# One core, a fused block of embedding, quantised attention, experts and local attention: pairs finished two at a time, a norm turned in two batches with the router's logits second, value moves by tile, and another order before the last projection

## What is computed

```python
h = tok(x)                                   # patches @ W.T + b, class token, positions
h = h + attn0(layernorm(h))                  # 4-bit input, ternary weights, 16 heads
h = h + ffn0(layernorm(h))                   # shared expert + top 2 of 8 experts
h = h + attn1(layernorm(h))                  # attention with a latent, then windowed attention
h = h + clip((layernorm(h) @ sign(w).T) * scale + bias, -100, 100)

def attn0(x):
    proj = quant4(x) @ ternary_weight(Wqkv_w).T + Wqkv_b
    ql, kl = rotary(q) @ U, rotary(k) @ U
    y = softmax(ql @ kl.T / sqrt(dk)) @ v
    return quant4(y) @ ternary_weight(Wo_w).T     # quant4: one scale per token

def ffn0(x):
    probs = softmax(x @ router_w + router_b)      # rw, ids = top 2, weights made to sum to 1
    y = sum over e of w_e * (silu(x @ gate_w[e]) * (x @ up_w[e])) @ down_w[e]
    return y + (silu(x @ sh_gate_w) * (x @ sh_up_w)) @ sh_down_w
```

## Time and profile before

| | |
|---|---|
| median of 3 runs | 330.63 us (328.04 to 330.92) |
| profiled execution | 332.31 us, span 330.3 us, 8349 instructions |
| busy share | PE 94%, PEld 79%, DVE 66%, ACT 49%, POOL 46% |
| chain that ended last | PE 60%, DVE 17%, SyncE's queue 8%, issue 5%, ACT 5%, DMA 2% |
| mean granted clock of TensorE | 0.967 of full |
| DMA | 36.74 MB, mean 111 GB/s |

### The profile page before, as it was taken

One profiled execution on the slowest core, in us unless ns is written; L12 is line 12 of the kernel. 1 busy time (PEld: TensorE's weight loads), 2 busy tenths in 40 slices (PEclk: granted clock), 3 DMA queues, 4 the chain that ended last, 5 costly groups with the idle time before them and its releaser, 6 DMA issues.

```text
span 330.3 us, 8349 instructions
## 1 busy us (share of the span) xinstructions
PE 309.3 (94%) x3406; PEld 260.3 (79%) x3408; DVE 217.0 (66%) x574; ACT 160.4 (49%) x353; POOL 153.1 (46%) x178
## 2 busy tenths in 40 slices
PE   7999999999898898999999999999699998999886
PEld 5775678876588888999999999999575676567765
DVE  1089898997877434455655545453577986898674
ACT  0304575556343135576667676763221694169410
POOL 1201209910334782698879888986582000410020
PEclk9999999998979979999999999999979999999987
DMA  7992001320021252537666566514800000000002
GB/s 267 403 396 92 3 0 57 127 99 2 1 96 50 89 167 83 177 127 240 212 221 203 183 217 206 196 34 119 269 4 0 3 9 5 2 1 9 5 2 73
DMA packets 18879, 36.74 MB, mean 111 GB/s; under 512 B 4602, under 2 KB 12849, under 8 KB 18840
## 3 DMA queue, kind: packets, MB, share of 16 engines
q1 hardware_dynamic: 17440, 33.35, 30.2%
q0 software_dynamic: 960, 2.43, 2.3%
q10 hardware_dynamic: 440, 0.41, 0.5%
HBM read 30.28 MB, written 5.75 MB: 109 GB/s over the span
## 4 chain that ended last, share of the span: by engine, by line
PE 60%; DVE 17%; SPq 8%; issue 5%; ACT 5%; DMA 2%; another core or an unknown queue 1%; POOL 1%; ACTq 0%; DVEq 0%; POOLq 0%
PE ps L1662 13%; PE ps L1663 11%; PE ps L1664 11%; SPq L465 8%; PE ps L1442 4%; PE ps L1860 3%; PE ps L1549 2%; PE ps L1454 2%; PE ps L1449 1%; DMA vo<-v_tok 1%; PE ps L1517 1%; PE ps L1561 1%; DVE stats L789 1%; PE ps L1824 1%; PE ps L1574 1%
## 5 line engine op out<-in xcount | busy, mean ns | idle before, releaser
L1339 POOL TENSOR_TENSOR w0l<-raw,w0h 128x384 fp32r<-128x384 f32 (+1 forms) x60 | 56.3, 975 | 15.7 <-ACT w0h L573 15.3
L1089 DVE TENSOR_TENSOR ps<-gact,ps 128x256 f32<-128x256 f32 (+3 forms) x60 | 26.2, 437 | 40.6 <-ACT gact L592 39.0
L1355 POOL TENSOR_TENSOR rstd<-vtmp,cst 128x3 f32<-128x3 f32 (+1 forms) x8 | 6.7, 840 | 91.3 <-DVE vtmp L799 46.3
L1339 POOL TENSOR_TENSOR w1l<-raw,w1h 128x384 fp32r<-128x384 f32 (+1 forms) x48 | 44.8, 971 | 6.5 <-ACT w1h L573 5.7
L592 ACT ACTIVATE gact<-ps 128x256 f32<-128x256 f32 (+3 forms) x60 | 23.2, 387 | 24.8 <-PE ps L1664 16.5
L1094 DVE TENSOR_TENSOR hrl<-ps,hrh 128x256 fp32r<-128x256 f32 (+1 forms) x48 | 20.3, 423 | 18.5 <-ACT hrh L596 17.6
L596 ACT ACTIVATE hrh<-ps 128x256 fp32r<-128x256 f32 (+1 forms) x48 | 18.5, 384 | 27.2 <-DVE ps L1089 26.0
L1662 PE MATMUL ps<-xg0h,w1h 128*128 128x256 f32 x88 | 25.8, 293 | 0.0
L1662 PE MATMUL ps<-xg1h,w0h 128*128 128x256 f32 x88 | 25.6, 291 | 0.0
L1442 PE MATMUL ps<-cst 128*128 128x512 f32 x54 | 25.3, 614 | 0.0
L1663 PE MATMUL ps<-xg1l,w0h 128*128 128x256 f32 x88 | 24.9, 283 | 0.0
(11 more groups left out here) (309 smaller groups left out, 898.7 us busy)
## 6 DMA issues: line engine op xcount, KB each, us to landing
raw<-in_wexp SPq DMA_DIRECT2D x18, 768.0 KB, 4.3
raw<-in_wexp SPq DMA_DIRECT2D x9, 640.0 KB, 4.4
xg_d<-zero SPq DMA_DIRECT2D x8, 256.0 KB, 10.7
xgs<-xg_d SPq DMA_DIRECT2D x8, 256.0 KB, 4.6
stage_l<-in_xT SPq DMA_DIRECT2D x6, 320.0 KB, 5.0
yg_d<-y SPq DMA_DIRECT2D x7, 256.0 KB
stage_l<-in_tokW SPq DMA_DIRECT2D x6, 128.0 KB, 5.0
stage_l<-in_wq SPq DMA_DIRECT2D x1, 512.0 KB, 5.2
```

The source lines that it names most:

```text
L1089: V.tensor_tensor(up, gact[i % 2][rows_of(c), 0:n], up, ALU.mult).then_inc(S("hm"), 1)
L1339: last = nc.gpsimd.tensor_tensor(wset[i][1][w], raw[w], wset[i][0][w].bitcast(F32), ALU.subtract)
```

## The change

1. Values: SyncE waits ahead of each part of a batch for the tile from which it is read, in place of one wait per group.
2. Pairs: `finish` takes two pairs at once for the pairs 0 to 5 (`FINISH`), so that the stream on VectorE is shift, shift, finish of two; the rounding stays one instruction a pair. The last two pairs are finished singly. The spare products are two instead of four. In the tail two spare products are put ahead of the row scales, and three spare products take the place of the keep-clock product.
3. Last projection: three biases, two keep-clock products, the transposes, three spare products, the fourth bias.
4. Norm of the shared products: turned into four banks (two batches by two halves); `xTh` and `xTl` are made batch by batch, first of all; the copies to `xnT` follow them. Unit 0 starts with the first batch. The logits stand behind unit 0, the position products behind unit 2.

```diff
@@ pe: pairs @@
-                    pe.wait_ge(S("y"), p - 1)
+                    pe.wait_ge(S("y"), p // 2)
...
-                for _ in range(4):
+                for _ in range(2):
...
                 turn_y(p)
-            pe.wait_ge(S("ma7"), PAIRS)
+            spare(2, 5)
+            pe.wait_ge(S("ma7"), len(FINISH))
...
             turn_y(PAIRS - 1)
-            keep_clock(1, 1)
+            spare(3, 5)
@@ vector: pairs @@
+            def finish(first, n):
+
+                done = FINISH.index((first, n)) + 1
+                pairs = slice(first, first + n)
+                dve.wait_ge(S("y_mm"), first + n)
+                yv = bank(6 + first % 2, n).rearrange("p (a c) -> p a c", a=n)[:, :, 0:H * VW].rearrange(
+                    "p a (j w) -> p a j w", w=VW)
+                z = rz[:, first % 2:first % 2 + n, :]
+                link(V.reciprocal(z, yv[:, :, :, DH]))
+                y = yq[:, pairs, :]
+                V.tensor_tensor(y.rearrange("p a (j w) -> p a j w", w=DH), yv[:, :, :, 0:DH],
+                                z.unsqueeze(3).to_broadcast([P, n, H, DH]), ALU.mult).then_inc(S("y"), 1)
+                dve.wait_ge(S("y"), done)
+                m = ma2[:, pairs]
+                link(V.tensor_reduce(m, y, AX_X, ALU.max, apply_absolute_value=True))
+                V.tensor_scalar(m, m, 1e-6, 1.0 / 7.0, ALU.max, ALU.mult).then_inc(S("ma7"), 1)
+                dve.wait_ge(S("ma7"), done)
+                link(V.reciprocal(rma[:, pairs], m))
+                for p in range(first, first + n):
+                    V.tensor_scalar(yq[:, p, :], yq[:, p, :], rma[:, p:p + 1], MAGIC, ALU.mult,
+                                    ALU.add).then_inc(S("yr"), 1)
+
+            for i in range(PAIRS // 2):
+                shift(2 * i)
+                shift(2 * i + 1)
+                if i >= 1:
+                    finish(2 * i - 2, 2)
+            finish(PAIRS - 2, 1)
+            finish(PAIRS - 1, 1)
@@ scalar: norm @@
-            act.wait_ge(S("nT_mm"), 1)
-            A(xnT[:, 0, :], bank(4, 2)[:, 0:TP], ACT.Copy).then_inc(S("nT0"), 1)
-            act.wait_ge(S("nT0"), 1)
-            act.wait_ge(S("nT1"), 1)
-            for k in range(DC):
-                A(xTh[:, k, :], xnT[:, k, :], ACT.Copy).then_inc(S("xTh"), 1)
+            for i in range(2):
+                act.wait_ge(S("nT_mm"), turned_upto(1, i))
+                for k in range(DC):
+                    A(xTh[:, k, cols_of(i)], first_turned(i, k), ACT.Copy).then_inc(S("xTh"), 1)
+            for i in range(2):
+                act.wait_ge(S("xTl"), DC * i + 1)
+                A(xnT[:, 0, cols_of(i)], first_turned(i, 0), ACT.Copy).then_inc(S("nT0"), 1)
@@ vector: norm @@
-            dve.wait_ge(S("nT_mm"), 1)
-            V.tensor_copy(xnT[:, 1, :], bank(6, 2)[:, 0:TP]).then_inc(S("nT1"), 1)
-            for k in range(DC):
-                dve.wait_ge(S("xTh"), k + 1)
-                V.tensor_tensor(xTl[:, k, :], bank(4 + 2 * k, 2)[:, 0:TP], xTh[:, k, :].bitcast(F32),
-                                ALU.subtract).then_inc(S("xTl"), 1)
+            for i in range(2):
+                for k in range(DC):
+                    dve.wait_ge(S("xTh"), DC * i + k + 1)
+                    V.tensor_tensor(xTl[:, k, cols_of(i)], first_turned(i, k), xTh[:, k, cols_of(i)].bitcast(F32),
+                                    ALU.subtract).then_inc(S("xTl"), 1)
+            for i in range(2):
+                V.tensor_copy(xnT[:, 1, cols_of(i)], first_turned(i, 1)).then_inc(S("nT1"), 1)
@@ pe: shared products @@
             transposes(1)
-            spare(4, 0)
-            pe.wait_ge(S("nT0"), 1)
-            pe.wait_ge(S("nT1"), 1)
...
+            def logits():
+                pe.wait_ge(S("nT0"), 2)
+                pe.wait_ge(S("nT1"), 2)
...
             for u in range(NH):
-                if u == 0:
-                    pe.wait_ge(S("xTl"), DC)
+                if u < 2:
+                    pe.wait_ge(S("xTl"), DC * (u + 1))
                 if u >= 2:
                     pe.wait_ge(S("hl"), u - 1)
                 shared_gate_up(u, u // 2, u % 2)
-                if u == 1:
+                if u == 0:
+                    logits()
+                if u == 2:
                     pe.wait_ge(S("sel"), 1)
@@ sync: values @@
-                    sp.wait_ge(S("v_tok"), (TT - MOVED) * li + grp + 2 - MOVED)
-                    if li == 0:
+                    if li == 0 and grp == 2:
                         sp.wait_ge(S("cleared"), 2)
                     for b in range(4 * grp, 4 * grp + 4):
                         for lo, hi in rows_of_batch(b):
+                            sp.wait_ge(S("v_tok"), (TT - MOVED) * li + lo // P + 1 - MOVED)
@@ pe: last projection @@
-            for t in range(4):
+            for t in range(3):
                 pe.wait_ge(S("bn"), TT * 4 + t + 1)
                 bias(t)
+            pe.wait_ge(S("bn"), TT * 4 + 4)
+            keep_clock(2, 3)
             transposes(4)
+            spare(3, 3)
+            bias(3)
```

## The result

The changed kernel took 335.65 us (median of 4 runs, 333.75 to 336.61), the kernel before 330.77 beside it: ratio 1.0154, 95% interval 1.0092 to 1.0217. It is slower, by less than 2%. Timed again in twelve executions on another chip it was slower by less: 328.44 against 326.01 us, ratio 1.0052 (1.0016 to 1.0088). I had forecast 326.8 us, 1% faster. Ratios and averages leave disturbed executions out and medians take all in, so that the two need not agree; three ratios (the short fallback, the old norm with four spare products the first time, the new order alone the first time) stand on 334.0 us for before, where its average beside them is 331.5, and there I go by the averages.

A forecast was written before the change was run, and what follows sets the result against it. VectorE paces the pair loop from pair 4 on, TensorE products the experts, TensorE the last projection. Terms -1.5 - 0.6 + 3.3 - 2.85 - 2.2 = -3.85 against the 330.63 us median give 326.8 us; 8-in-10 range 322.5 to 331.

The forecast's parts named there:

- ScalarE's stall: 4.92 us idle before a SiLU near the scatters: shorter gives 323.5 us, chance 0.18; longer gives 330, chance 0.12.
- Pairs, -1.5: Pair loop: joined finishes save VectorE time, less a hole no longer filled and later values; -1.5 us, bounds -0.7 and -2.2.
- the clock falls inside the pair loop: Rival: fewer spare products and waits for joined divisions halve TensorE's clock; three such pairs give 335.5 us; chance 0.06.
- Tail, -0.6: End of the pair loop: short spare products finish before the copy, so the first output projection isn't held up; -0.6 us.
- Norm and router, +3.3: Norm before the shared products: reordering delays router and position products, hence the scatters; +3.3 us, bounds +1.9 and +3.3.
- Router +1.4: VectorE's first router operation begins at 95.6 instead of 94.18, since the logits come later; +1.4 us.
- Position products behind a half-clock unit 2, +1.9: After 4 us of TensorE idle time unit 2 runs at half clock, so VectorE waits 1.9 us for the position products.
- Values, -2.85: Both local-attention layers: group 2's DMA queue starts earlier, ending TensorE's waits; -1.6 and -1.25 us, bounds -2.3 and -3.0.
- Last projection, -2.2: Final projection: TensorE at full clock, then VectorE sets 0.88 us a tile; last clip at 325.2 instead of 327.34, -2.2 us.
- The clock in the last projection: Rival: the clock goes down there all the same, turning the 2.2 us gain into +0.5; 329.5 us, chance 0.14.

The follow-up runs named there:

- the short fallback: Changed kernel with most products cut from TensorE's never-entered code for experts given more rows than fit: 330.96 us, before 333.70, ratio 0.9886.
- the one with the gap filled: Changed kernel with filler restoring the branch's place and ten spare products in TensorE's idle time ahead of the third shared unit: 325.02 us, ratio 0.9980.
- 34 earlier in before: Kernel before with fewer, equivalent spare products, so its branch lies 34 TensorE instructions earlier, as in the changed kernel: 333.55 us, before 333.70, ratio 1.0037.
- 222 later: Kernel before with 222 more TensorE instructions ahead of its branch, small products replacing three keep-clock products: 332.29 us, before 326.37, ratio 1.0208.

## Why the prediction was wrong

**What failed** is the way in which the sum was made: I counted what each edit does to engines, queues and waits, and not that fewer instructions move everything behind them in the stream. It is a term that is absent from the sum, 2.4 us at the branch (2.2 to 2.8) and 0.8 to 1.4 in the values. Of the 5.6 us between the forecast (-3.85) and the twelve executions (+1.7) these two are 3.4; the rest is the clock in the pair loop, 0.9, and gains that were put too high, as below. I had the Trainium skill's section on fetching before me and used it on ScalarE's stall only, where it settled nothing.

- **Pairs, -1.5.** Right in mechanism where the clock holds, and near in size in half of those profiles: -1.3 in three, -0.4 to -0.9 in three. But "the clock falls inside the pair loop" was a rival at 0.06 and is there in 3 of 9 profiles, for up to 4.1 us against a full-clock loop (33.27 against 29.2). The reason against it, "TensorE stays busy for over nine tenths of each round", was wrong: it had been busy 1.61 of 2.00 us in 62 to 64 here, and 1.01 in 68 to 70 in the second timing, the latter just before the clock fell.
- **Tail, -0.6.** The change did what I said, 0.90 for 1.57 us. But the half clock of rows 3 and 5 was chance: five other kernels with the old tail have 6.49 us in that stage, as the new one has. Worth 0.
- **Norm and router, +3.3.** Router +1.4: measured +1.38. Position products behind a half-clock unit 2, +1.9: measured +1.4 (1.2 to 2.2 in others), and shown by the run that moved them back. Unit 2 didn't start cold, as the sum had it, but fell to half clock a microsecond in. Nor is the fall in rows 5 the kind that I took it for: TensorE had been busy from 92.0 to 93.7, without a break, when it came. Sum +2.8 at the scatters. Not foreseen: in four profiles unit 0 itself ran cold, and the router came another 1.3 us later (3.4 in the one with the gap filled).
- **Values, -2.85.** -1.5 and -0.2 to -1.1 in the stages; mechanism right, the second layer over-sized.
- **Last projection, -2.2.** -1.8 against this profile, from the clock, as forecast; against others of the old form 0.8 to 2.0, by how long their clock was down; VectorE's pace of 0.8 a tile from 325.08 on, and one wait more than I allowed at the last tile (0.42).
- **Rivals.** ScalarE's stall stayed where it was and nearly as long (4.42 and 4.92); on two other chips no kernel of either kind has it. The clock in the last projection held. So neither decided anything. In the old order on the slower chips the stage to the first expert took 37.9 to 38.9 us with ScalarE's stall and 37.9 in the one profile without.

Put together with what was measured: -1.3 + 2.8 + 2.4 + 1.0 - 2.3 - 1.8 = +0.8, and a third of 2.8 for the clock in the loop, +1.7 with it: what the twelve executions gave. That it fits to the tenth is luck, since several of the terms vary by a microsecond from profile to profile. The 4.9 us of the first four are not accounted for beyond this, apart from 1.4 us of half clock in the first expert in the profiled one, which two other kernels showed as well and most didn't.

**Still open:** why the new order alone loses 3.6 us in its stage and 1.0 to 2.5 in all; why the stretch ahead of the pair loop takes 47.5 to 51.4 us from profile to profile, with no change in it but filler; why 34 earlier in before cost less than 222 later; what ScalarE waits for near the scatters.

## What to carry to other kernels

If a kernel has a branch, count the instructions ahead of it on each engine before and after an edit, however far away the edit is; read the stage at the branch even though nothing there was changed, ask the trace how long the branch instruction itself took, and look in the DMA rows for when the instruction blocks were fetched. Cheap filler or a shorter skipped body is worth a try when an edit that should win doesn't and the branch has grown. And don't thin out products that only keep the clock up because one profiled execution stayed up: read several profiles.

## What the runs showed of the hardware

- A taken branch took TensorE 0.35 to 0.45 us in fourteen profiles, which cost nothing visible (0.65 us from the start of ScalarE's copy to the product, as long as the copy), and 3.43 to 3.91 in four, which cost 2.2 to 2.8 us, by its place in the stream and the length of the jump.
- The stream also ran dry in straight code, in runs of small products: 0.7 to 1.15 us of idle weight loads some 35 us behind the branch, seven products from the end of a group, in all four profiles that stalled at the branch, 1.14 and 0.82 us in two that didn't, and 0.5 to 0.7 three times in the changed kernel without a branch.
- Chips differ more than the change did: before had medians of 326.0 and 326.4 us on two chips and 332.4 to 333.7 on three, and an idle time of ScalarE without a known releaser, 2.3 to 4.9 us ahead of a SiLU near the scatters or near the last expert, is in eight of the twelve profiles of the slower chips and in none of the eight of the faster ones.
